# Windowed attention layers on one core: values spread through device memory, the band on small tiles, and new orders on three engines

## Chip, core and metric

The kernel runs on one core of a Trainium2 chip. The metric is device time in microseconds (us). Five engines run side by side, each in the order of its own program, and wait for one another by semaphores: TensorE (PE; its weight loads are listed as PEld), VectorE (DVE), ScalarE (ACT), GpSimd (POOL) and SyncE (SP), which issues the transfers.

## What is computed

2048 tokens of 128 channels go through a time-mixing layer with a norm, and then through six layers of windowed attention and a gated feed-forward net, all in float32, with a last norm behind:

```python
for i in range(DEPTH):                                    # 6
    x = attn_layer(shift_tokens(x), Wqkv[i], q_scale[i], k_scale[i], Wo[i]) + x
    x = ffn_layer(shift_tokens(x), ln_g[i], ln_b[i], W1[i], b1[i], W2[i], b2[i]) + x

def attn_layer(x, Wqkv, qs, ksc, Wo):                     # 16 heads of 64
    q, k, v = split(x @ Wqkv)
    q = l2norm(q) * qs;  k = l2norm(k) * ksc
    q = q * cos * scale + rotate_half(q) * sin * scale
    k = k * cos * inv   + rotate_half(k) * sin * inv
    # windows of 32 tokens; a query sees its own window and the one before
    sim = where(mask, -max, einsum('bhwie,bhwje->bhwij', bq, bk2) * 8)
    out = einsum('bhwij,bhwje->bhwie', softmax(sim), bv2)
    return out @ Wo
```

`bk2` and `bv2` hold, for each window of 32, the 32 tokens before it and its own 32: each key and value is wanted in two places.

## The kernel before

The tokens are cut into 16 tiles of 128. `layers` runs 96 tile-layers as a software pipeline. In step `s` four tiles are under way: `p = s + 1` (projections, norms of q and k, rotation), `a = s` (transposes of q and k, scores, softmax), `b = s - 1` (product with the values, output projection), and, for a pair of tiles in two steps, the feed-forward net. A step is **even** or **odd** by `s`: an odd step starts with the gating (`gelu`, `hidden`) and ends with the narrowing (`xa`) and the deviation of the norm (`dev_made`, line 1363); an even step ends with the norm's transposes (line 1372) and the widening (line 1262). Steps 7 to 94 are a loop of 44 rounds, each an odd and an even step.

Every engine's order is written out by hand in its own `step` function; nothing is scheduled by a tool. Operands pass through four pairs of PSUM banks: `bank_a` (queries, then values, of `p`), `bank_b` (keys, then the feed-forward), `bank_s` (probabilities, product with the values, output projection) and `bank_t` (transposes of q and k, scores). In the profile they are named `proj_a`, `proj_b`, `att`, `turn`.

The steps that the prediction follows:
- TensorE, in this order: probabilities turned (1246, `att<-identity,probs`), query projection (1278), key projection (1293), q transposes (1246, `turn<-identity,rotated`), product with the values (1312), k transposes (1246), `heads_out` turned (1246), the band (1332) and on top of it the scores (1338), value projection (1350), and behind it what is left of the step, with the output projection (1379).
- VectorE: sum of the masses (1187), in odd steps `hidden` (1196), the two sums of squares (1155), `heads_out` (1161), the inverse root (nine operations on 128x32, lines 88 to 104), `unit[0]` and `unit[1]` (1180), the two centrings of the scores (1169 and 1172), `xa` (1219), `xb` (1223), `var_f` (1228), `along[1]` (1233).
- GpSimd: `turns`, the shifted inputs, then `across[0]` (999), `along[0]` (1032), `rotated[0]` (1006), `across[1]`, in odd steps `rstd_f` (1040), `rotated[1]`. The k transposes of the next step wait for `rotated[1]`.
- ScalarE: the evacuations `p_t`, `q_t`, `k_t`, `o_t`, the squares, the value copy `val` (1114) and the exponentials (1061, `weigh`).
- SyncE: `spread(m, odd)` copies the values of tile `m` from `v_tok` (in the profile `val`) into `v_win`, where each window has its two blocks of 32 tokens, with sixteen transfers of 32 rows (lines 945 and 948). The next layer's weights are loaded from the same queue, between the spreads.

The band is a mask of 0 and -1e30 in bfloat16, 64 columns for each of the 16 heads, which TensorE writes into the scores' banks by a product with the identity; the first tile of the sequence has a mask of its own.

Of the kernel before, what the change touches and what calls it, by code (L numbers as in the profile page):

```python
# [23 lines left out]
F32 = mybir.dt.float32  # L24
# [101 lines left out]
def build(nc, x, vectors, mix_w1, mix_w2, decay_w1, decay_w2, r_weights, r_norm, wqkv, wo, ffn, qk_scales,  # L126
          positions, carry, ident, band, level_masks, out):
    with ExitStack() as ctx:
# [688 lines left out]
def layers(nc, ctx, given):  # L817
# [10 lines left out]
    passed = given["passed"]  # L828

    with ExitStack() as own:  # L830
# [44 lines left out]
        eps_set = sem("eps_set")  # L875
        cleared, centre_made = sem("cleared"), sem("centre_made")
# [12 lines left out]
        v_laid, v_spread = sem("v_laid"), sem("v_spread")  # L889
        scored, maxed, centred, weighed = sem("scored"), sem("maxed"), sem("centred"), sem("weighed")  # L890
# [39 lines left out]
        with nc.Block() as block:  # L930
            @block.sync
            def _(sp):
                def spread(m, odd):

                    now, old = v_tok[odd], v_tok[1 - odd]
                    sp.wait_ge(v_laid, m + 1)
                    stand_alone(sp, passed)
                    after(sp, mixed, 2 * (m - 1))
                    stand_alone(sp, passed)
                    for par in range(2):  # L940
                        base = 2 * WINDOW * par
                        own_rows = slice(base + WINDOW, base + 2 * WINDOW)
                        flat = [v[:, par, :, :].rearrange("p a e -> p (a e)") for v in (now, old)]
                        for w in range(BLOCKS):
                            sp.dma_start(v_win[odd][own_rows, w, :],
                                         flat[0][WINDOW * w:WINDOW * w + WINDOW, :]).then_inc(v_spread, 16)
                            before = flat[0][WINDOW * (w - 1):WINDOW * w, :] if w else flat[1][TILE - WINDOW:TILE, :]
                            sp.dma_start(v_win[odd][base:base + WINDOW, w, :], before).then_inc(v_spread, 16)
# [6 lines left out]
                sp.wait_ge(cleared, 2)  # L955
                for m in range(5):
# [90 lines left out]
            def _(act):  # L1047
                def step(s, h, odd, live):
# [8 lines left out]
                    def weigh(par):  # L1057
                        act.wait_ge(centred, 2 * a + par + 1)
# [20 lines left out]
                    if live["a"]:  # L1079
                        for j in range(2):  # L1080
# [3 lines left out]
                                .then_inc(q_laid, 1)  # L1084
                    if live["a"]:
# [5 lines left out]
                    if live["down"]:  # L1091
                        after(act, warmed, h)
                        act.activation(warm[:, :], ones[:, 0:1], ACT.Exp).then_inc(warmed, 1)
# [454 lines left out]
```

## Time and profile before

| | |
|---|---|
| median of 3 runs | 2002.96 us (2001.11 to 2008.23) |
| profiled execution, its own time | 2001.63 us |
| its span, first to last instruction | 1999.8 us |
| mean granted TensorE clock | 0.975 |
| busy: PE / DVE / ACT / POOL | 1771.6 / 1543.1 / 1156.1 / 1454.8 us |
| share of the span | 89% / 77% / 58% / 73% |

The first 195 us are the time-mixing layer, the last 15 us the last norm; in between are the 96 tile-layers, and from 262 us to about 1955 us the pairs of steps repeat. The chain of work that ended last covers only the last norm, 1% of the span, so it doesn't tell what sets the pace of the layers: the waits and the timeline of one pair do. In a timeline row the columns are start, duration, engine, line, operation, result and operands, count; in brackets stands the idle time of the engine just before, and what ended it. The duration of several matrix products in one row reaches to the end of the last one, which overlaps the next row's start. "issue" means that no releaser is seen.

### The profile page before, as it was taken

The page shows a single profiled execution, that of the slowest core. Times are in us where ns is not written, and L with a number is a line of the kernel's source. Part 1 is how long each engine was busy: PE and PEld are TensorE (multiplying, and loading weights), DVE is VectorE, ACT ScalarE, POOL GpSimd, SP SyncE. Part 2 cuts the span into 40 slices and gives each one's busy share as a digit, 9 for nine tenths or more (in the row PEclk, how much of TensorE's full clock was granted, in tenths as well). Part 3 has the DMA queues.
Part 4 walks back from the last instruction along what each step waited for, and adds up shares of the span by engine and source line. Part 5 has one row for each costly group of instructions (what it writes and reads, how often), then busy time and mean ns, then how long its engine had stood idle before and what let it go on. Part 6 is the DMA issues. An engine that isn't in the chain of part 4 may idle for free. (4 is left out here: it accounts for less than half of the span.)

```text
span 1999.8 us, 85355 instructions
## 1 busy us (share of the span) xinstructions
PE 1771.6 (89%) x34184; PEld 1277.4 (64%) x34184; DVE 1543.1 (77%) x2729; ACT 1156.1 (58%) x1966; POOL 1454.8 (73%) x967
## 2 busy tenths in 40 slices
PE   7764789999999999999999999999999999999995
PEld 3453466666666666666666666666666666666664
DVE  4774798778878877788788777887887788778864
ACT  2311456666666666666666666666666666666663
POOL 3221787787788778877887787778777877887771
PEclk9985899999999999999999999999999999999998
DMA  4000222223232223222223322233222232322220
GB/s 151 2 3 1 56 63 57 64 60 84 66 74 58 54 55 94 63 68 58 63 56 85 76 67 55 52 81 81 62 58 62 61 86 63 74 60 52 55 63 22
DMA packets 93581, 123.43 MB, mean 62 GB/s; under 512 B 27760, under 2 KB 41808, under 8 KB 93392
## 3 DMA queue, kind: packets, MB, share of 16 engines
q1 hardware_dynamic: 93232, 122.42, 24.3%
q8 instruction: 46, 0.75, 0.2%
q10 hardware_dynamic: 288, 0.13, 0.0%
q14 instruction: 15, 0.12, 0.0%
HBM read 20.74 MB, written 1.05 MB: 11 GB/s over the span
## 5 line engine op out<-in xcount | busy, mean ns | idle before, releaser
L999 POOL TENSOR_TENSOR across<-unit,turns 128x1024 f32<-128x1024 f32 x192 | 497.4, 2591 | 275.5 <-issue 265.6
L1006 POOL TENSOR_TENSOR rotated<-along,across 128x1024 f32<-128x1024 f32 x192 | 495.7, 2582 | 14.2
L1155 DVE TENSOR_REDUCE sums<-squares 128x16 f32<-128x1024 f32 x192 | 234.0, 1219 | 177.9 <-ACT squares L1054 177.7
L1246 PE MATMUL turn<-identity,rotated 128*128 128x128 f32 x1536 | 204.7, 276 | 35.5 <-POOL rotated L1006 34.3
L1246 PEld LDWEIGHTS turn<-identity,rotated 128*128 128x128 f32 x1536 | 172.3, 141 | 98.0 <-issue 82.5
L1032 POOL TENSOR_TENSOR along<-unit,turns 128x1024 f32<-128x1024 f32 x96 | 228.0, 2375 | 0.0
L1350 PE MATMUL proj_a<-w_qkv,shift_a 128*128 128x512 f32 x384 | 189.5, 616 | 36.3 <-DVE unit L1180 30.1
L1114 ACT COPY val<-proj_a 128x1024 f32<-128x1024 f32 x96 | 97.2, 1012 | 180.7 <-PE proj_a L1350 180.7
L1379 PE MATMUL att<-o_t,w_o 128*128 128x128 f32 x1536 | 188.9, 277 | 0.0
L1278 PE MATMUL proj_a<-w_qkv,shift_a 128*128 128x512 f32 x384 | 184.4, 603 | 5.0 <-POOL shift_a L989 3.7
L1379 PEld LDWEIGHTS att<-o_t,w_o 128*128 128x128 f32 x1536 | 181.0, 193 | 1.0 <-issue 1.0
L1089 ACT COPY k_t<-turn 128x512 f32<-128x512 f32 x192 | 103.2, 589 | 134.5 <-PE turn L1246 134.5
L1293 PE MATMUL proj_b<-w_qkv,shift_a 128*128 128x512 f32 x384 | 180.9, 593 | 0.0
L1233 DVE TENSOR_TENSOR along<-unit,turns 128x1024 f32<-128x1024 f32 x96 | 165.7, 1726 | 0.0
L1054 ACT ACTIVATE squares<-proj_a 128x1024 f32<-128x1024 f32 x96 | 98.2, 1023 | 115.8 <-PE proj_a L1278 115.8
L1312 PE MATMUL att<-v_win,p_t 64*32 64x64 f32 x12288 | 154.2, 225 | 0.8 <-ACT p_t L1074 0.8
L1338 PEld LDWEIGHTS turn<-k_t,q_t 64*32 64x32 f32 x12288 | 128.3, 105 | 41.4 <-issue 41.1
L1074 ACT COPY p_t<-att 128x512 f32<-128x512 f32 x192 | 103.1, 589 | 89.0 <-PE att L1246 89.0
L1312 PEld LDWEIGHTS att<-v_win,p_t 64*32 64x32 f32 x12288 | 135.6, 105 | 20.1 <-issue 16.9
L1161 DVE TENSOR_TENSOR heads_out<-att,inv_mass 128x512 f32<-128x512 f32 x192 | 123.6, 686 | 31.4 <-PE att L1312 31.4
L1338 PE MATMUL turn<-k_t,q_t 64*32 64x64 f32 x12288 | 144.2, 225 | 0.0
L1172 DVE TENSOR_TENSOR logits<-turn,row_max 128x512 f32<-128x512 f32 x192 | 132.8, 692 | 6.7
(201 smaller groups left out, 3366.2 us busy)
## 6 DMA issues: line engine op xcount, KB each, us to landing
v_win<-val SPq DMA_DIRECT2D x1536, 64.0 KB, 2.0
w_qkv<-wqkv_dram SPq DMA_DIRECT2D x18, 512.0 KB, 3.9
w_o<-wo_dram SPq DMA_DIRECT2D x6, 512.0 KB, 4.7
where<-positions_dram SPq DMA_DIRECT2D x1, 2048.0 KB, 10.7
w_ffn<-ffn_dram SPq DMA_DIRECT2D x12, 170.5 KB, 2.3
w_ffn<-ffn_dram SPq DMA_DIRECT2D x6, 192.0 KB, 2.3
x_tok<-x_dram SPq DMA_DIRECT2D x4, 256.0 KB, 4.2
out_dram<-final SPq DMA_DIRECT2D x4, 256.0 KB, 2.4
```

The source lines that it names most:

```text
L999: pool.tensor_tensor(a[:, :, ::-1, :], u, table, ALU.mult).then_inc(acrossed[j], 1)
L1006: pool.tensor_tensor(rotated[j][:, :, :], along[j][:, :, :], across[j][:, :, :], ALU.add).then_inc(rotated_in[j], 1)
L1032: pool.tensor_tensor(along[0][:, :, :], unit[0][:, :, :], turns[mine][:, 0, :].unsqueeze(1).broadcast_to([128, HEADS, HEAD]), ALU.mult).th ...
L1155: dve.tensor_reduce(sums[:, j, :], squares[j][:, :, :], AX.X, ALU.add).then_inc(summed[j], 1)
L1233: dve.tensor_tensor(along[1][:, :, :], unit[1][:, :, :], turns[mine][:, 2, :].unsqueeze(1).broadcast_to([128, HEADS, HEAD]), ALU.mult).the ...
L1246: mm = pe.transpose(bank[:, TILE * (i % 4):TILE * (i % 4) + TILE], buffer[:, TILE * i:TILE * i + TILE], identity[:, :])
L1278: mm = pe.matmul(bank_a[:, half, :], shift_a[mine][:, :], w_qkv[:, 512 * half:512 * half + 512], start=True, stop=True)
L1293: mm = pe.matmul(bank_b[:, half, :], shift_a[mine][:, :], w_qkv[:, base:base + 512], start=True, stop=True)
L1312: mm = pe.matmul(bank_s[WINDOW * w:WINDOW * w + WINDOW, par, HEAD * a_:HEAD * a_ + HEAD], p_t[rows, a_, WINDOW * w:WINDOW * w + WINDOW], v ...
L1338: mm = pe.matmul(bank_t[WINDOW * w:WINDOW * w + WINDOW, par, HEAD * a_:HEAD * a_ + HEAD], q_t[rows, a_, WINDOW * w:WINDOW * w + WINDOW], k ...
L1350: pe.matmul(bank_a[:, par, :].rearrange("p (a e) -> p a e", a=PAIRS), shift_a[mine][:, :], values[:, par, :, :], start=True, stop=True).th ...
L1379: mm = pe.matmul(bank_s[:, 0, 0:TILE], w_o[:, a_, :], o_t[:, a_, :], start=(a_ == 0), stop=(a_ == PAIRS - 1))
```

## The change

- **Values.** `spread` writes the tile's values to a buffer in device memory, `v_rows` (32 + 2 x 128 rows, the odd tile's last 32 rows also at its top), waits until they are there, and reads them back with four transfers of 128 rows (of two heads' halves, near and own window) in place of the sixteen. A write waits until all reads of the spread before it have landed.
- **Band.** Eight products on tiles of 64 rows and 32 columns in place of two on 128x128. In even steps ScalarE first copies the mask in question into `band_now`, so that no address depends on a register; the mask for the first tile is laid out for both row halves.
- **Orders.** TensorE: the query projection goes ahead of the turned probabilities, the product with the values ahead of the q transposes, the output projection and the norm's transposes ahead of the value projection, the deviation ahead of the narrowing. VectorE: `heads_out` between the two sums of squares, `centre_scores(1)` between `unit[0]` and `unit[1]`, then `centre_scores(0)`; `along[1]` ahead of `xa` and `var_f`. ScalarE: `o_t` right behind `k_t`, then `norm_tok` and the table load; `weigh(1)` first, the value copy just ahead of `weigh(0)`.

The step range, the tiles under way in a step and the buffers' numbers stay. GpSimd's code is the same.

On TensorE, an even step ahead of the loop, before:

```order
L1246 MATMUL att<-identity,probs 128x128 x8
L1278 MATMUL proj_a<-w_qkv,shift_a 128x512 x2
L1293 MATMUL proj_b<-w_qkv,shift_a 128x512 x2
L1246 MATMUL turn<-identity,rotated 128x128 x8
L1312 MATMUL att<-v_win,p_t 32x64 x64
L1246 MATMUL turn<-identity,rotated 128x128 x8
L1246 MATMUL att<-identity,heads_out 128x128 x8
L1332 MATMUL turn<-band_bf,identity_bf 128x512 x2
L1338 MATMUL turn<-k_t,q_t 32x64 x64
L1350 MATMUL proj_a<-w_qkv,shift_a 128x512 x2
L1372 MATMUL att<-identity,norm_tok 128x128 x2
L1379 MATMUL att<-o_t,w_o 128x128 x8
```

The same step on TensorE in the changed kernel (its line numbers are its own):

```order
L1295 MATMUL proj_a<-w_qkv,shift_a 128x512 x2
L1269 MATMUL att<-identity,probs 128x128 x8
L1316 MATMUL proj_b<-w_qkv,shift_a 128x512 x2
L1327 MATMUL att<-v_win,p_t 32x64 x64
L1269 MATMUL turn<-identity,rotated 128x128 x16
L1269 MATMUL att<-identity,heads_out 128x128 x8
L1360 MATMUL turn<-band_now,identity_bf 32x512 x8
L1368 MATMUL turn<-k_t,q_t 32x64 x64
L1379 MATMUL att<-o_t,w_o 128x128 x8
L1388 MATMUL att<-identity,norm_tok 128x128 x2
L1396 MATMUL proj_a<-w_qkv,shift_a 128x512 x2
```

The product with the values is now the fourth group instead of the fifth, the output projection stands ahead of the value projection, and the query projection starts the step.

On VectorE, the end of the same step, from `unit[0]` on, before:

```order
L1180 TENSOR_TENSOR unit<-proj_a,inv_norm 128x1024
L1180 TENSOR_TENSOR unit<-proj_b,inv_norm 128x1024
L1169 TENSOR_REDUCE row_max<-turn 128x8
L1172 TENSOR_TENSOR logits<-turn,row_max 128x512
L1169 TENSOR_REDUCE row_max<-turn 128x8
L1172 TENSOR_TENSOR logits<-turn,row_max 128x512
L1223 TENSOR_TENSOR xb<-att,xa 128x128
L1233 TENSOR_TENSOR along<-unit,turns 128x1024
```

And in the changed kernel:

```order
L1201 TENSOR_TENSOR unit<-proj_a,inv_norm 128x1024
L1190 TENSOR_REDUCE row_max<-turn 128x8
L1193 TENSOR_TENSOR logits<-turn,row_max 128x512
L1201 TENSOR_TENSOR unit<-proj_b,inv_norm 128x1024
L1190 TENSOR_REDUCE row_max<-turn 128x8
L1193 TENSOR_TENSOR logits<-turn,row_max 128x512
L1242 TENSOR_TENSOR xb<-att,xa 128x128
L1248 TENSOR_TENSOR along<-unit,turns 128x1024
```

One centring has moved between the halves; behind them nothing moved in an even step.

The rest of the diff, cut to its core:

```diff
+    v_rows = nc.dram_tensor("v_rows", (WINDOW + 2 * TILE, INNER), F32, kind="Internal").ap()
...
                 def spread(m, odd):
-                    now, old = v_tok[odd], v_tok[1 - odd]
+                    at = WINDOW + TILE * odd
+                    flat = v_tok[odd][:, :, :, :].rearrange("p b a e -> p (b a e)")
                     sp.wait_ge(v_laid, m + 1)
                     stand_alone(sp, passed)
+                    after(sp, v_spread, 64 * m)
+                    stand_alone(sp, passed)
+                    sp.dma_start(v_rows[at:at + TILE, :], flat).then_inc(v_written, 16)
+                    if odd:
+                        sp.dma_start(v_rows[0:WINDOW, :], flat[TILE - WINDOW:TILE, :]).then_inc(v_tail, 16)
+                    sp.wait_ge(v_written, 16 * m + 16)
+                    stand_alone(sp, passed)
+                    if not odd:
+                        sp.wait_ge(v_tail, 8 * m + 16)
+                        stand_alone(sp, passed)
                     after(sp, mixed, 2 * (m - 1))
                     stand_alone(sp, passed)
                     for par in range(2):
-                        base = 2 * WINDOW * par
...
-                        for w in range(BLOCKS):
-                            sp.dma_start(v_win[odd][own_rows, w, :],
-                                         flat[0][WINDOW * w:WINDOW * w + WINDOW, :]).then_inc(v_spread, 16)
-                            before = flat[0][WINDOW * (w - 1):WINDOW * w, :] if w else flat[1][TILE - WINDOW:TILE, :]
-                            sp.dma_start(v_win[odd][base:base + WINDOW, w, :], before).then_inc(v_spread, 16)
+                        for near in range(2):
+                            base = 2 * WINDOW * par + WINDOW * near
+                            row = TILE * odd + WINDOW * near
+                            sp.dma_start(v_win[odd][base:base + WINDOW, :, :],
+                                         v_rows[row:row + TILE, 512 * par:512 * par + 512]
+                                         .rearrange("(w p) f -> p w f", p=WINDOW)).then_inc(v_spread, 16)
...
                     def weigh(par):
-                        act.wait_ge(centred, 2 * a + par + 1)
+                        act.wait_ge(centred, 2 * a + 2 - par)
...
+                    if live["a"] and not odd:
+                        which = (0 if a % TILES == 0 else 1) if isinstance(a, int) else (tile_of(a) + 15) // 16
+                        after(act, scored, 2 * (a - 1))
+                        act.copy(band_now[:, :], band_bf[:, which, :]).then_inc(band_set, 1)
...
                         act.wait_ge(v_projected, 2 * p + 2)
-                        after(act, v_spread, 256 * p)
+                        after(act, v_written, 16 * (p - 1))
+                        if mine:
+                            act.wait_ge(v_tail, 8 * (p - 1) + 16)
                         act.copy(v_tok[mine][:, :, :, :], ...).then_inc(v_laid, 1)
...
+                        band = (band_bf[:, mask_other, :] if odd else band_now[:, :]).unsqueeze(1)\
+                            .broadcast_to([128, PAIRS, 2 * WINDOW])
+                        if not odd:
+                            pe.wait_ge(band_set, a // 2 + 1 if isinstance(a, int) else h + 4)
                         pe.wait_ge(k_laid, 2 * a + 2)
-                        for par in range(2):
-                            pe.matmul(bank_t[:, par, :].rearrange("p (a c) -> p a c", a=PAIRS), identity_bf[:, :], band,
-                                      start=True, stop=False, skip_group_check=True)
+                        stand_alone(pe, passed)
+                        for w in range(BLOCKS):
+                            for par in range(2):
+                                rows = slice(HEAD * par, HEAD * par + HEAD)
+                                at = HEAD * par + (WINDOW if w else 0)
+                                pe.matmul(bank_t[WINDOW * w:WINDOW * w + WINDOW, par, :]
+                                          .rearrange("p (a c) -> p a c", a=PAIRS),
+                                          identity_bf[rows, at:at + WINDOW], band[rows],
+                                          start=True, stop=False, skip_group_check=True)
...
-    first = hidden | ((a < WINDOW) & (c < WINDOW))
+    first = hidden | ((a % (2 * WINDOW) < WINDOW) & (c < WINDOW))
```

## Rows read from the trace of the kernel before

**Rows 1.** Windows, 42 repeating pairs: start:end, length, busy time (count) of each engine.

```profile
core 0: us, PE busy (x) PEld busy (x) DVE busy (x) ACT busy (x) POOL busy (x), PEclk, DMA share, GB/s
334.22:1865.00 1530.78, 1424.52 (x27715) 1038.01 (x27714) 1231.82 (x2142) 969.27 (x1636) 1228.15 (x799) 1.00 0.27 66
```

**Rows 2.** Waits of TensorE in that stretch: us in total, times, longest.

```profile
PE proj_a L1350 <- DVE unit L1180: 27.1, 81, 0.5
PE att L1246 <- issue: 26.2, 42, 0.6
PE turn L1246 <- POOL rotated L1006: 23.8, 42, 0.6
```

**Rows 3.** Timeline of TensorE, one pair from an even step's k transposes.

```profile
1016.03 1.09 PE L1246 MATMUL turn<-identity,rotated 128*128 128x128 f32 x8 [0.58 <-POOL rotated L1006]
...
1018.04 0.60 PE L1332 MATMUL turn<-band_bf,identity_bf 128*128 x2
1018.57 1.48 PE L1338 MATMUL turn<-k_t,q_t 64*32 64x64 f32 x128
1020.28 1.96 PE L1350 MATMUL proj_a<-w_qkv,shift_a 128*128 128x512 f32 x4 [0.23 <-DVE unit L1180]
...
1022.29 1.95 PE L1379 MATMUL att<-o_t,w_o 128*128 128x128 f32 x16
1024.40 1.99 PE L1262 MATMUL proj_b<-normed,w_ffn 128*128 128x256 f32 x8 [0.16 <-ACT normed L1122]
...
1027.10 1.04 PE L1246 MATMUL att<-identity,probs 128*128 128x128 f32 x8
1027.97 1.88 PE L1278 MATMUL proj_a<-w_qkv,shift_a 128*128 128x512 f32 x4
1029.69 1.88 PE L1293 MATMUL proj_b<-w_qkv,shift_a 128*128 128x512 f32 x4
...
1032.37 1.62 PE L1312 MATMUL att<-v_win,p_t 64*32 64x64 f32 x128
...
1052.47 1.09 PE L1246 MATMUL turn<-identity,rotated 128*128 128x128 f32 x8 [0.56 <-POOL rotated L1006]
```

**Rows 4.** Timeline of VectorE in the same pair.

```profile
1026.00 1.21 DVE L1187 TENSOR_REDUCE mass<-probs 128x16 f32<-128x1024 f32 x1
...
1028.25 0.47 DVE L1196 SCALAR_TENSOR_TENSOR hidden<-turn,w_ffn,gelu 85x256 f32<-85x256 f32 x1
...
1034.18 1.29 DVE L1161 TENSOR_TENSOR heads_out<-att,inv_mass 128x512 f32<-128x512 f32 x2 [0.30 <-PE att L1312]
1035.39 0.18 DVE L88 SCALAR_TENSOR_TENSOR sums_min<-sums 128x32 f32<-128x32 f32 x1
...
1037.56 1.22 DVE L1180 TENSOR_TENSOR unit<-proj_a,inv_norm 128x1024 f32<-128x1024 f32 x1
...
1042.47 0.47 DVE L1219 SCALAR_TENSOR_TENSOR xa<-proj_b,w_ffn,xb 128x256 f32 x1
...
1045.13 1.98 DVE L1233 TENSOR_TENSOR along<-unit,turns 128x1024 f32<-128x1024 f32 x1
```

**Rows 5.** Timeline of GpSimd in two neighbouring odd steps.

```profile
1009.56 3.34 POOL L999 TENSOR_TENSOR across<-unit,turns 128x1024 f32<-128x1024 f32 x1
...
1043.68 2.36 POOL L1006 TENSOR_TENSOR rotated<-along,across 128x1024 f32<-128x1024 f32 x1
```

**Rows 6.** Timeline of ScalarE, the copies of the turned probabilities.

```profile
1027.73 1.07 ACT L1074 COPY p_t<-att 128x512 f32<-128x512 f32 x2
```

**Rows 7.** Groups by line in that stretch: busy us, mean ns, idle before, releaser.

```profile
L1155 DVE TENSOR_REDUCE sums<-squares 128x16 f32<-128x1024 f32 x168 | 204.9, 1220 | 149.1 <-ACT squares L1054 149.1
```

**Rows 8.** Timeline early in the layers, a root operation beside GpSimd.

```profile
235.83 0.66 DVE L88 SCALAR_TENSOR_TENSOR sums_min<-sums 128x32 f32<-128x32 f32 x1
...
235.70 0.74 POOL L1017 TENSOR_TENSOR turns<-where,scales 128x256 f32<-128x256 f32 x1
```

**Rows 9.** Transfers by line: count, KB each, median us from issue to landing.

```profile
x_tok<-x_dram SPq DMA_DIRECT2D x4, 256.0 KB, 4.2
out_dram<-final SPq DMA_DIRECT2D x4, 256.0 KB, 2.4
```

## What I predict, and why

> **What bounds the kernel now.** I read the windows first. In the stretch of 42 identical pairs of steps, 1530.78 us long, TensorE is busy 93% at a granted clock of 1.00, VectorE and GpSimd 80% each [rows 1]. One pair takes 36.45 us. Then the waits of TensorE in that stretch [rows 2]. It waits little, but in every step: the value projection for VectorE's first normalised half (27.1 us, 81 times), the turning of the probabilities at the head of an even step (26.2, 42 times), the k transposes of an even step for GpSimd (23.8, 42 times). So this is not one full engine but rings of work across engines that close every pair. The timeline shows the ring that matters here [rows 3 to 5]:
> - the k transposes of an even step start at 1016.03 and the next (odd) step starts at 1027.10: **R** = 11.07 us on TensorE;
> - from that start to the end of `unit[0]` on VectorE, 1037.56 + 1.22 = 1038.78: **X** = 11.68 us;
> - from there GpSimd's five large operations run back to back, and the next even step's k transposes start at 1052.47: **P** = 13.69 us.
>
> R + X + P = 36.44 us, which is the pair. A second ring is as tight: `unit[0]` releases the value projection, behind which everything up to the next step's start waits in TensorE's order. The first ring has about 0.2 us of slack to the second, the 0.23 us that the value projection waits at 1020.28. An edit pays only if both rings get shorter.
>
> **The change, part by part.**
>
> *TensorE's order.* The output projection and the norm's transposes move between the scores and the value projection. The second ring is cut: `unit[0]` now has some 2 us more before the value projection asks for it, and the probabilities turn behind the query projection (1.72 us, 1027.97 to 1029.69), which covers their wait for `xb`. What is late next is the first ring, so I price that one.
>
> R, from the rows of the even step [rows 3]: 11.07 less the value projection's wait of 0.23, and less the wait of the widening behind the output projection. From 1022.29 to 1024.40 are 2.11 us, while the output projection streams as many columns (16 x 128) as the value projection does (4 x 512), 1.75 us or a little over; I take 0.36 off, with 0.16 (what the row itself shows as idle) as the other end. The band gives back some more, next. The added standing-alone waits and the wait for `band_set` find their semaphores set long before (a 64-column copy on ScalarE, issued while it waits for the k transposes): nothing, or 0.1 us.
>
> *The band on small tiles.* Two 128x128 products of 512 columns take 0.53 us (1018.04 to 1018.57). Now there are eight of the same length on 64x32 tiles, two row halves by four column quarters. If they ran one after another they would take 8 x 0.26 = 2.1 us. The scores, on the same tiles, say that they don't: 128 records of 64 columns take 1.48 us, while at the output projection's pace (1.75 us for 2048 columns) they would take 7.0 us, so 4.7 run at a time. Eight by that share are 0.45 us, all eight at once 0.27 us. I take 0.30, nearer to the second, since the long streams leave time to load the next weights: 0.23 off. Ends: 0.27 and 2.1 us. The Trainium skill, "TensorE: Matmul & The Clock Gate", Part 3 (Measured speedup vs the span model), gives packed tiles the length of one product and about 4 ns for each further one, here an estimate of 0.24 us; by it R would be 0.06 us shorter.
>
> So R becomes 11.07 - 0.23 - 0.36 - 0.23 = 10.25 us.
>
> X, from the first instruction of the odd step, now the query projection: it takes 1.72, the turned probabilities 0.87 (1027.10 to 1027.97), the key projection 1.72; so the product with the values starts at 4.31, if `p_t` is there: ScalarE starts those copies 0.63 after the turning starts and takes 1.07 [rows 6], 1.72 + 0.63 + 1.07 = 3.42, in time. `heads_out` starts 1.81 after that product (1032.37 to 1034.18), at 6.12. From `heads_out` to `unit[0]` were 3.38 us; now the second sum of squares stands between, 1.22 [rows 7]. `unit[0]` ends at 6.12 + 3.38 + 1.22 + 1.22 = 11.94. X grows by 0.26: products come earlier, but a whole reduction moved behind them.
>
> P stays 13.69: GpSimd's code is untouched, and `along[1]` on VectorE still falls into its run. The rows show how these two collide: `along`, issued at 1045.13, ends 1.07 us after GpSimd's operation from 1043.68 ends, and an operation of GpSimd that starts under it takes 3.34 instead of 2.36 us [rows 4, 5]. That 1 us is in P before and after.
>
> Sum: 10.25 + 11.94 + 13.69 = 35.88 against 36.44, **0.56 us a pair**. The other parity's ring (odd to odd) has some 1.5 us of room: TensorE's odd remainder loses its waits too, and GpSimd's run there has no `rstd` in it.
>
> *VectorE's order.* With `centre_scores(1)` between the halves, `unit[1]` comes 1.3 us later; GpSimd needs it only after three operations (7 us). In an even step the k transposes now wait longer for GpSimd (about 2 us), so the nine small root operations meet GpSimd's last large one. The trace has that case at the start of the layers: the first root operation took 0.66 instead of 0.18 us, to the end of GpSimd's 0.74 us operation [rows 8]. Here this costs the even X 0.5 to 1.4 us, inside the room of that parity's ring. The Trainium skill, "SBUF — State Buffer", Who interferes with whom, states it as an exclusive lock between a VectorE instruction with two SBUF inputs and GpSimd; the trace agrees with 0.66 us. `xa` and `var_f` move behind `along[1]`, about 2 us later; `rstd` is asked for after GpSimd's fourth operation and `xa` by the next key projection, 0.4 us after it is there by my count. Nothing, with little margin.
>
> *ScalarE's order.* `o_t` ahead of `norm_tok` and of the table load, `weigh(1)` first, the value copy one place later: ScalarE has waits in every step, and the value copy must end before the next query projection. By the sum it does, with 0.4 us to spare. The q transposes now stand right before the k transposes, whose bank waits for the q copies: about 0.3 us, in the even step under GpSimd's wait, in the odd one in that ring's room.
>
> *Values by way of device memory.* Sixteen transfers of 64 KB become a write of 512 KB, in odd tiles a tail of 128 KB, a wait for both, and four reads of 256 KB. No row has this route. A 256 KB write took 2.4 us and a 256 KB read 4.2 us [rows 9]: the write up to 4.8, the reads at best side by side 4.2, at worst in series 16.8; 9 to 22 us with the issues. The value copy ends about 1 us after the projection's 1022.2; its product stands just ahead of the k transposes at 1052.47, some 27 us later. Hidden at either end, and SyncE has fewer issues than before. At the five layer changes the weights of the next layer queue behind the reads instead of behind sixteen issues: 0 to 2 us each. The Trainium skill, "DMA: Bandwidth & Descriptors", Anatomy of one DMA, speaks against such a detour: it names device memory the slowest target to confirm a write. No run here shows that alone.
>
> **Sum over the run.** About 46 pairs have the full work (42 in the stretch and two at either side); 46 x 0.56 = 26 us. The start of the layers and the drain I leave as they are, 3 us either way. The profiled execution took 2001.63 us (span 1999.8), so 1976; the median of the runs shown is 1.3 us above it: **1977 us**. The bounds of the terms (band 0.27 to 0.53, widening 0.16 to 0.36, X up to 0.3 either way) put the pair between 35.5 and 36.2, so 1960 to 1992.
>
> **Rivals.**
> - *Nothing left over.* The first ring had only 0.2 us of slack, so if the band keeps 0.5 us, the output projection needs its 2 us and the odd root also meets GpSimd's copies (0.3 us), the ring is again 36.4 to 36.6: 2000 to 2010. For it: X really does grow. Against: three waits on TensorE vanish.
> - *VectorE's tail misses its gap (slower).* In an even step `along[1]` is ready 4.91 (both centrings and both halves, 1037.56 to 1042.47) + 0.3 for `xb` = 5.2 us after `unit[0]` starts; GpSimd's third operation starts at 6.1 (1043.68). If it is later than that, from 0.9 us more on, it waits that operation out, to 8.5, and ends at 9.5; the sum of masses, the reciprocal and the gating follow, 2.72 (1026.00 to 1028.72), and only then may the odd key projection overwrite its bank, at 12.3. From it to the next `unit[0]` are 1.72 + 1.81 + 3.38 + 1.22 = 8.1, then 1.22 + 13.69, and some 2.5 of root work after GpSimd's end: 37.8 us a pair, 62 us more: 2065. For it: VectorE is 80% full and each of these waits is new. Against: 0.9 us are left.
> - *The small tiles run in series.* 1.2 to 1.8 us on R, which also uses up those 0.9 us: 37.4 to 38, 2045 to 2075. Against it: the scores' 4.7 at a time.
> - *The detour takes longer than a step.* Each write waits for the last reads to land, so past 18 us a step it sets the pace; at 22 us 43 a pair, 2300. Only reads in strict series do that.
> - *More room than counted.* If GpSimd and VectorE collide less, the pair falls to 35.2 or so: 1945.
>
> **How the numbers follow.** Forecast 63%; nothing left over 17%; the missed gap 8%; tiles in series 5%; the detour 2%; more room 5%. A measurement of this kernel tells about 0.5% (10 us) from no change. Faster by more: the forecast nearly whole and the last case, 67%. Within: 18%. Slower: 15%. The range leaves out the slow cases and the fastest: 1953 to 2012; the forecast's own is 1960 to 1992.
>
> **What would show it.** The value projection's and the turned probabilities' waits gone; the even k transposes waiting about 2 us for GpSimd and nothing else large on TensorE; a pair of 35.9 us; `heads_out` starting 6.1 us after the query projection; eight band products within 0.3 us; `along[1]` ending before GpSimd's `rotated[0]` begins in even steps. The forecast is wrong if the odd key projection waits for `hidden`, if the product with the values waits for a transfer, or if the even root ends so late that the other parity's ring sets the pair.

## The result

| | changed | before |
|---|---|---|
| median | 2070.78 us (2061.48 to 2072.32, 4 runs) | 2005.58 us (2001.11 to 2008.23, 4 runs) |
| span of the profiled execution | 2070.1 us | 1999.8 us |
| mean granted TensorE clock | 0.934 | 0.975 |

The changed kernel takes 1.0311 times the time of the one before (95% interval 1.0284 to 1.0337): it is **slower**. The forecast was 1977 us with a range of 1953 to 2012, faster at 0.67.

The starts of the key projections give a ledger of the 70.3 us between the two spans. They are counted from 0: number n makes the keys of tile n, and "step n" in this ledger and in the texts below means its start, although it runs in step n - 1 of the kernel's own count. Numbers 11 and 93, first in the changed kernel, then in the one before:

```profile
415.37 1.88 PE L1316 MATMUL proj_b<-w_qkv,shift_a 128*128 128x512 f32 x4
1955.73 1.88 PE L1316 MATMUL proj_b<-w_qkv,shift_a 128*128 128x512 f32 x4
```

```profile
391.03 1.88 PE L1293 MATMUL proj_b<-w_qkv,shift_a 128*128 128x512 f32 x4
1886.99 1.88 PE L1293 MATMUL proj_b<-w_qkv,shift_a 128*128 128x512 f32 x4
```

Up to step 0 are 8.3 us (206.5 instead of 198.2; the kernels below lie between 199 and 208 us there, for a reason that is not known). Steps 0 to 11 take 208.9 us instead of 192.8, 16.1 more. The 41 pairs from step 11 to step 93 take 1540.4 instead of 1496.0, 44.4 more (37.57 us a pair instead of 36.49 on average; most pairs of the kernel before take 36.46). The rest is 1.5. So there are two losses to explain, the pairs and the start. Every kernel has one profiled execution, so how much these parts vary from one execution to the next is not known.

**The pair.** Page of the changed kernel, groups of instructions (busy, mean ns; idle before, and releaser):

```profile
L1269 PE MATMUL turn<-identity,rotated 128*128 128x128 f32 x1536 | 241.5, 307 | 112.6 <-POOL rotated L1021 94.6
L1248 DVE TENSOR_TENSOR along<-unit,turns 128x1024 f32<-128x1024 f32 x96 | 224.7, 2341 | 0.0
L1316 PE MATMUL proj_b<-w_qkv,shift_a 128*128 128x512 f32 x384 | 184.3, 602 | 23.2 <-DVE hidden L1217 23.2
```

TensorE's waits have gathered in one place: 94.6 us for GpSimd ahead of the k transposes, 2.1 us in every even step, where there were several of at most 0.6 us in a pair [rows 2, 3]. The key projection waits for `hidden`, and `along` takes 2.34 us on average. The timeline of TensorE in one pair, changed kernel:

```profile
1019.69 1.09 PE L1269 MATMUL turn<-identity,rotated 128*128 128x128 f32 x8
1022.87 1.67 PE L1269 MATMUL turn<-identity,rotated 128*128 128x128 f32 x8 [2.08 <-POOL rotated L1021]
1024.33 1.91 PE L1269 MATMUL att<-identity,heads_out 128*128 128x128 f32 x8
1026.17 0.61 PE L1360 MATMUL turn<-band_now,identity_bf 64*32 64x512 bf16 x8
1026.58 1.50 PE L1368 MATMUL turn<-k_t,q_t 64*32 64x64 f32 x128
...
1034.42 1.88 PE L1295 MATMUL proj_a<-w_qkv,shift_a 128*128 128x512 f32 x4
1036.13 1.04 PE L1269 MATMUL att<-identity,probs 128*128 128x128 f32 x8
1037.71 1.95 PE L1316 MATMUL proj_b<-w_qkv,shift_a 128*128 128x512 f32 x4 [0.54 <-DVE hidden L1217]
```

Behind the wait the same eight transposes that took 1.09 us [rows 3] take 1.67, and those of `heads_out` 1.91 instead of 1.09, which the kernel before has here:

```profile
1016.98 1.09 PE L1246 MATMUL att<-identity,heads_out 128*128 128x128 f32 x8
```

The windows of these stretches say why (the column ahead of the DMA share is the granted clock):

```profile
1020.80:1022.80 2.00, 0.00 (x0) 0.00 (x0) 1.90 (x3) 0.80 (x3) 2.00 (x2) 1.00 0.90 180
1022.87:1024.33 1.46, 1.46 (x8) 1.46 (x9) 1.36 (x4) 0.59 (x1) 1.10 (x3) 0.62 0.01 3
1024.33:1026.17 1.84, 1.84 (x9) 1.51 (x8) 1.67 (x6) 1.17 (x2) 0.03 (x1) 0.50 0.00 0
1026.17:1028.02 1.85, 1.85 (x138) 1.55 (x137) 0.39 (x1) 1.18 (x3) 1.32 (x1) 0.87 0.00 0
1028.02:1034.42 6.40, 6.40 (x39) 4.99 (x36) 6.21 (x7) 3.93 (x6) 6.32 (x4) 1.00 0.02 10
```

TensorE idles, and then the granted clock falls to 0.50, the 1.2 GHz of its two levels, through the transposes and into the band. Before, it was 1.00 over the whole stretch [rows 1]. All 41 steady pairs of the changed kernel have this fall; the waits of 2.08 us behind them, at 1962.13 and 1997.58, have none. What it does further is on VectorE and GpSimd, same pair:

```profile
1028.14 0.69 DVE L1190 TENSOR_REDUCE row_max<-turn 128x8 f32<-128x512 f32 x1 [1.57 <-PE turn L1368]
...
1032.12 2.79 DVE L1248 TENSOR_TENSOR along<-unit,turns 128x1024 f32<-128x1024 f32 x1
```

```profile
1031.47 2.36 POOL L1021 TENSOR_TENSOR rotated<-along,across 128x1024 f32<-128x1024 f32 x1
```

VectorE waits 1.57 us for the late scores, `along[1]` is issued 0.65 us after `rotated[0]` has begun and ends 1.08 us behind its end, `hidden` is late, and the odd key projection waits 0.54 us. That is the slow rival's ring, at 37.57 us instead of its 37.8, but its trigger is the clock. So the first theory: **the gathered wait costs the clock, and the clock makes `along[1]` miss its gap.**

### The profile page after: what moved, and what is told of

Same layout as the page of the kernel before. It is cut to its first block and busy times, and to the rows that moved or that the text cites. A ratio compares the mean times of both kernels' runs of the same rounds, so it can differ in the third digit from the quotient of the medians.

```text
span 2070.1 us, 86199 instructions
## 1 busy us (share of the span) xinstructions
PE 1812.0 (88%) x34760; PEld 1319.7 (64%) x34760; DVE 1629.7 (79%) x2729; ACT 1181.2 (57%) x2014; POOL 1452.0 (70%) x967
## 5 line engine op out<-in xcount | busy, mean ns | idle before, releaser
L1269 PE MATMUL turn<-identity,rotated 128*128 128x128 f32 x1536 | 241.5, 307 | 112.6 <-POOL rotated L1021 94.6
L1269 PEld LDWEIGHTS turn<-identity,rotated 128*128 128x128 f32 x1536 | 185.4, 153 | 148.1 <-issue 108.3
L1248 DVE TENSOR_TENSOR along<-unit,turns 128x1024 f32<-128x1024 f32 x96 | 224.7, 2341 | 0.0
L1190 DVE TENSOR_REDUCE row_max<-turn 128x8 f32<-128x512 f32 x192 | 131.3, 684 | 84.6 <-PE turn L1368 84.6
L1379 PE MATMUL att<-o_t,w_o 128*128 128x128 f32 x1536 | 196.8, 281 | 0.0
L1295 PE MATMUL proj_a<-w_qkv,shift_a 128*128 128x512 f32 x384 | 182.7, 598 | 9.9 <-ACT val L1143 6.2
L1396 PE MATMUL proj_a<-w_qkv,shift_a 128*128 128x512 f32 x384 | 182.4, 597 | 6.1 <-issue 6.1
L1076 ACT ACTIVATE probs<-logits 128x512 f32<-128x512 f32 x192 | 121.4, 632 | 104.8 <-DVE logits L1193 104.7
L1327 PEld LDWEIGHTS att<-v_win,p_t 64*32 64x32 f32 x12288 | 127.4, 105 | 83.1 <-issue 83.1
L1098 ACT COPY q_t<-turn 128x512 f32<-128x512 f32 x192 | 103.2, 589 | 104.9 <-PE turn L1269 104.9
L1368 PEld LDWEIGHTS turn<-k_t,q_t 64*32 64x32 f32 x12288 | 143.6, 108 | 18.5 <-issue 14.3
```

The lines of the kernel that those rows point to most:

```text
L1190: dve.tensor_reduce(row_max[:, heads], scores, AX.X, ALU.max).then_inc(maxed, 1)
L1248: dve.tensor_tensor(along[1][:, :, :], unit[1][:, :, :], turns[mine][:, 2, :].unsqueeze(1).broadcast_to([128, HEADS, HEAD]), ALU.mult).the ...
L1269: mm = pe.transpose(bank[:, TILE * (i % 4):TILE * (i % 4) + TILE], buffer[:, TILE * i:TILE * i + TILE], identity[:, :])
L1295: mm = pe.matmul(bank_a[:, half, :], shift_a[mine][:, :], w_qkv[:, 512 * half:512 * half + 512], start=True, stop=True)
L1368: mm = pe.matmul(bank_t[WINDOW * w:WINDOW * w + WINDOW, par, HEAD * a_:HEAD * a_ + HEAD], q_t[rows, a_, WINDOW * w:WINDOW * w + WINDOW], k ...
L1379: mm = pe.matmul(bank_s[:, 0, 0:TILE], w_o[:, a_, :], o_t[:, a_, :], start=(a_ == 0), stop=(a_ == PAIRS - 1))
```

## Experiments

Each kernel is told by its edit; "changed" is the kernel after the change. Times are medians; ratios are to the kernel before, on the same chip.

**1. The wait filled** (changed):

```diff
+                    if live["a"] and not odd:
+                        pe.wait_ge(q_laid, 2 * a + 1)
+                        for i in range(12):
+                            pe.transpose(bank_t[:, 0, 0:TILE], identity[:, :], identity[:, :])
                     if live["a"]:
                         pe.wait_ge(rotated_in[1], a + 1)
```

> The changed kernel, with twelve more transposes (the identity by the identity, into the bank that the k transposes then overwrite) ahead of the k transposes of every even step, where TensorE otherwise waits 2.1 us for GpSimd. They add work and take nothing away. Theory (the new orders gather TensorE's waits into one, and behind it the granted clock falls to 1.2 GHz through the k transposes, the heads_out transposes and the band): the granted clock stays at 1.00, R falls from 11.55 to 10.0 to 10.3 us, along[1] gets back ahead of rotated[0], the key projection no longer waits for hidden, a pair takes 35.5 to 36.2 us, and the time is 1975 to 2010 us. Rival A (VectorE's new order misses its gap by itself; the clock only follows): the clock may stay up, but the key projection still waits for hidden and the pair stays above 37 us: 2040 to 2070. Rival B (the detour or the small band tiles slow TensorE): as the changed kernel, 2065 to 2075.

1984.76 us, 0.9889 (0.9854 to 0.9924), as the theory had it. TensorE in an even step, then `along[1]` on VectorE and `rotated[0]` on GpSimd:

```profile
1025.47 1.53 PE L1343 MATMUL turn<-identity 128*128 128x128 f32 x12 [0.24 <-ACT q_t L1098]
1027.25 1.09 PE L1269 MATMUL turn<-identity,rotated 128*128 128x128 f32 x8 [0.25 <-POOL rotated L1021]
1028.18 1.04 PE L1269 MATMUL att<-identity,heads_out 128*128 128x128 f32 x8
...
1037.18 1.88 PE L1295 MATMUL proj_a<-w_qkv,shift_a 128*128 128x512 f32 x4
```

```profile
1034.91 2.00 DVE L1248 TENSOR_TENSOR along<-unit,turns 128x1024 f32<-128x1024 f32 x1
```

```profile
1035.90 3.23 POOL L1021 TENSOR_TENSOR rotated<-along,across 128x1024 f32<-128x1024 f32 x1
```

The window of its steady stretch has the clock at 1.00:

```profile
418.00:1850.00 1432.00, 1393.24 (x27695) 1032.11 (x27694) 1247.62 (x2063) 946.51 (x1617) 1177.70 (x769) 1.00 0.39 102
```

The same orders, with work added, take 35.43 us a pair; `along[1]` is back at 2.00 us and starts 0.99 us ahead of `rotated[0]`, and no wait for `hidden` is left. Rival A falls: VectorE's order does not miss its gap by itself.

**2. Half the wait filled** (the same with six):

> The filled wait with six transposes instead of twelve: some 0.8 us of the 2.1 us are filled, in its first half, and about 1 us stays idle ahead of the k transposes. Theory (what brings the clock down is one long wait; waits of 1 us, as here and in the kernel with the heads_out transposes ahead, don't): clock at 1.00, pair 35.4 to 35.5 us, 1978 to 1995 us. Rival C (what counts is the idle time, so that half of it still brings the clock down at the worst moments): some pairs of 36.5 to 37.6 us, 2000 to 2060 us.

1989.98 us, 0.9925 (0.9898 to 0.9951); pair 35.43 us, clock 1.00. A wait of 0.88 to 0.92 us ahead of the k transposes is harmless here: none of 42 has the fall.

**3. The wait cut in two, no work added** (changed): the transposes of `heads_out` ahead of the k transposes.

```diff
+                    if live["b"]:
+                        pe.wait_ge(scaled_out, 2 * b + 2)
+                        for j in range(2):
+                            transposes(bank_s[:, j, :], heads_flat, j, o_turned)
                     if live["a"]:
                         pe.wait_ge(rotated_in[1], a + 1)
...
-                    if live["b"]:
-                        pe.wait_ge(scaled_out, 2 * b + 2)
-                        for j in range(2):
-                            transposes(bank_s[:, j, :], heads_flat, j, o_turned)
```

> The changed kernel with one exchange in TensorE's order: the transposes of heads_out stand ahead of the k transposes, so that TensorE's one wait of 2.1 us in the even step is cut into two, about 0.6 us for heads_out and 0.9 us for GpSimd. No work is added. Theory: no single long wait, so the granted clock stays at 1.00; the band then waits for the k copies (0.4 to 0.6 us), R 10.2 to 10.6 us, pair 35.7 to 36.3 us, 1975 to 2010 us. Rival A (VectorE's order alone): the key projection still waits for hidden, 2040 to 2070 us. Rival C (the clock falls by the sum of idle time in a step, however it is cut): the clock falls as in the changed kernel, 2055 to 2085 us.

2000.89 us, 0.9971 (0.9951 to 0.9991). The steady part is as expected, 35.65 us a pair at a clock of 1.00 with waits of 0.2 to 0.8 us. TensorE in an even step:

```profile
1033.60 1.09 PE L1269 MATMUL att<-identity,heads_out 128*128 128x128 f32 x8 [0.34 <-DVE heads_out L1182]
1034.89 1.09 PE L1269 MATMUL turn<-identity,rotated 128*128 128x128 f32 x8 [0.20 <-POOL rotated L1021]
1036.76 0.41 PE L1360 MATMUL turn<-band_now,identity_bf 64*32 64x512 bf16 x8 [0.77 <-issue]
```

The waits add up to 1.3 us here, where the changed kernel has one of 2.1. So the wait was cut and also became shorter, and rival C is weakened but not excluded. The start is another matter: this kernel's steps 0 to 11 took 222.7 us, 30 more than before, and used the gain up. Experiments 1 and 2 lost 24 and 21 us there. The start is taken up in 9 and 10.

**4. The detour undone** (changed; `spread` and its waits as before):

> The changed kernel with the values spread as before, by sixteen transfers from SBUF to SBUF; everything else as changed. Theory: the detour is hidden, so nothing moves: clock lower in the even k transposes as in the changed kernel, pair 37.5 us, 2060 to 2075 us. Rival A: the same. Rival B (the detour's traffic is what slows TensorE): the clock or the rates of the transposes come back, 1975 to 2010 us.

2016.6 us, 1.0037 (1.0017 to 1.0057). The theory said "nothing moves", and 54 us went. Was it the detour after all? The k transposes of four even steps in a row:

```profile
992.88 1.60 PE L1255 MATMUL turn<-identity,rotated 128*128 128x128 f32 x8 [1.83 <-POOL rotated L1009]
1030.75 1.91 PE L1255 MATMUL turn<-identity,rotated 128*128 128x128 f32 x8 [1.96 <-POOL rotated L1009]
1068.64 1.09 PE L1255 MATMUL turn<-identity,rotated 128*128 128x128 f32 x8 [1.96 <-POOL rotated L1009]
1104.12 1.09 PE L1255 MATMUL turn<-identity,rotated 128*128 128x128 f32 x8 [1.97 <-POOL rotated L1009]
```

Here the clock falls behind only 16 of 42 such waits, all of 1.8 to 2.0 us. A pair with the fall takes 37.9 us, one without 35.6. A wait of 1.79 us (at 556) has the fall and one of 2.03 us (at 813) has not, so the length of the wait alone does not decide. The changed kernel's slow pair is 0.3 us shorter (its product with the values ends earlier), and I formed a second theory: the fall comes at moments of its own, and a slow pair of 37.57 us happens to bring every next wait to such a moment again. In the changed kernel the k transposes do lengthen slowly, from 1.33 us at 421.77 to 1.97 us at 1624: the fall slides through them by 0.02 us a pair.

**5. More work in the slow pair** (changed):

```diff
                         pe.wait_ge(v_spread, 64 * b + 64)
                         stand_alone(pe, passed)
+                        if odd:
+                            for i in range(2):
+                                pe.transpose(bank_s[:, 0, 0:TILE], identity[:, :], identity[:, :])
```

> The changed kernel with two more transposes (identity by identity, 0.27 us, into the bank that the product then overwrites) ahead of the product with the values in every odd step, behind the key projection that waits for hidden: it adds work to the ring of a slow pair, like the 0.3 us by which that product is later without the detour, and takes nothing away. Theory (the clock falls behind the 2 us wait only if the wait meets it at the right moment; the changed kernel's slow pair of 37.57 us happens to bring every wait to the same moment): a slow pair takes 37.8 to 37.9 us, the next wait comes at another moment, and only some of the pairs are slow, as without the detour: 2015 to 2045 us, faster by added work. Rival D (the length of the wait alone decides, so that every pair is slow): every pair 37.84 us, 2078 to 2090 us.

2038.66 us, 1.0148 (1.012 to 1.0177): 32 us less than the changed kernel, by adding work. Slow pairs take 37.8 us, and the clock falls behind 24 of 42 waits of 2.1 us:

```profile
1083.80 1.82 PE L1269 MATMUL turn<-identity,rotated 128*128 128x128 f32 x8 [2.08 <-POOL rotated L1021]
1121.59 1.96 PE L1269 MATMUL turn<-identity,rotated 128*128 128x128 f32 x8 [2.09 <-POOL rotated L1021]
1159.40 1.09 PE L1269 MATMUL turn<-identity,rotated 128*128 128x128 f32 x8 [2.08 <-POOL rotated L1021]
```

Rival D falls. Of two equal waits one costs the clock and the next does not, and how often it happens has changed with the pair's length. What sets the moments is not shown.

**6. Both: wait filled, detour undone** (edits 1 and 4):

> Both edits of the earlier runs together: the twelve transposes in the even step's wait, and the values spread by sixteen transfers from SBUF to SBUF. Theory (the detour costs nothing in the steady stretch beyond what the clock does, and some 10 us in the first steps of the run, where TensorE waits for instructions): every pair 35.6 to 35.7 us, the key projection of step 11 some 10 us earlier than with the filled wait alone, 1970 to 1985 us. Rival B (the detour itself costs what undoing it gave, 54 us): 1930 to 1945 us.

1980.09 us, 0.985 (0.982 to 0.988); 35.64 us a pair. Without the wait, undoing the detour gives 5 us, not 54, and in the pairs it loses 0.2 us. Rival B falls.

**7. Each part alone.** The detour alone (before, with `spread` and its waits as changed):

> The kernel before with the values spread by way of device memory and nothing else of the change. Theory: TensorE's waits stay short and the clock at 1.00; the product with the values ends 0.2 to 0.3 us earlier, which the second ring takes back in part (0 to 0.2 us a pair), and the first ten steps lose 8 to 20 us: 1998 to 2022 us. Rival B (the detour costs 54 us): 2050 to 2065 us.

1987.24 us, 0.9888 (0.9856 to 0.992): better than the theory. The steady pair is 36.00 us against 36.46. In the kernel before, the product with the values takes 1.6 us and `heads_out` waits for it [rows 3, 4]; with the detour (first TensorE, then VectorE):

```profile
1035.96 1.49 PE L1327 MATMUL att<-v_win,p_t 64*32 64x64 f32 x128
```

```profile
1036.25 1.22 DVE L1170 TENSOR_REDUCE sums<-squares 128x16 f32<-128x1024 f32 x1 [0.32 <-ACT squares L1067]
1037.46 1.29 DVE L1176 TENSOR_TENSOR heads_out<-att,inv_mass 128x512 f32<-128x512 f32 x2
```

The product is 0.1 us shorter and `heads_out` starts 1.50 us behind its start instead of 1.81, waiting for nothing. Why the product runs faster was not settled; but in the steady stretch of all ten kernels with the detour it takes 1.48 to 1.49 us, and in the five without it 1.52 to 1.80.

The small band tiles alone (before, with the eight products and `band_now`):

> The kernel before with the band on small tiles and nothing else of the change. Theory (the small tiles give back 0.3 us a step, of which the first ring passes on what the second ring leaves it, 0.2 us, and the detour is not needed for it): clock at 1.00, pair 36.1 to 36.3 us, 1988 to 2002 us. Rival (the eight small products come in series): 2040 to 2075 us.

2012.32 us, 1.0026 (1.001 to 1.0043). The scores follow 0.23 us behind the band instead of 0.53, and the pair stays at 36.47 us, where the theory had 36.1 to 36.3. TensorE's waits from 420 to 1850 us:

```profile
PE proj_a L1363 <- DVE unit L1186: 49.5, 79, 0.8
PE att L1252 <- issue: 24.3, 39, 0.6
PE turn L1252 <- POOL rotated L1008: 22.1, 39, 0.6
```

The value projection's wait doubles, from 25.1 us in the same stretch before: the second ring takes all of it.

The small band tiles undone (changed, with two products of 128x128):

> The changed kernel with the band again as two products of 128x128 per step; everything else as changed. Theory: the small tiles give back what was counted, 0.2 to 0.3 us in each step at full clock, twice that behind the wait of the even step, and the clock still falls: 2070 to 2095 us. Rival B (the small tiles cost the time): 1975 to 2010 us. Rival A: 2070 to 2095 us.

2060.57 us, 1.0258 (1.0228 to 1.0288), below the 2070 to 2095 expected. The clock falls in 40 of 41 pairs, and the slow pair is 37.57 us to the hundredth as with them: in a slow pair the ring runs over `along[1]` and `hidden`, and the band does not lie on it.

**8. The orders alone** (changed, with edits 4 and the band undone):

> The changed kernel with the detour and the small band tiles undone: the new orders alone. Theory (the orders make the 2 us wait, and the clock falls behind some of the waits, with a slow pair near 37.9 us as without the detour): full-clock pairs of 35.9 to 36.1 us, at least a quarter of the pairs slow, 2010 to 2040 us. Rival B (detour and band bring the fall of the clock, the orders alone don't): clock at 1.00 in the steady stretch, 1980 to 2000 us.

2033.33 us, 1.0129 (1.0092 to 1.0166). The wait is there and the clock falls behind 27 of 43; pairs of 36.1 and 37.9 us. So the orders bring it, without the other two parts.

**9. The start: the first eleven tiles spread from SBUF to SBUF**, the later ones through device memory, on the kernel of experiment 1. `spread_near` holds the sixteen transfers of before, and SyncE waits there until they have landed; for the eleventh tile it also writes the values to device memory, for the first later one:

```diff
-                for m in range(5):
-                    spread(m, m % 2)
-                with sp.Fori(0, 5) as i:
-                    spread(i * 2 + 5, 1)
-                    spread(i * 2 + 6, 0)
+                for m in range(11):
+                    spread_near(m, m % 2)
+                with sp.Fori(0, 2) as i:
+                    spread(i * 2 + 11, 1)
+                    spread(i * 2 + 12, 0)
```

> The changed kernel with the filled wait, and with the first eleven tiles of values spread from SBUF to SBUF as before; from the twelfth on by device memory. Theory (in the first ten steps the detour's transfers delay the loading of instructions): the key projection of step 11 comes 8 to 18 us earlier than with the filled wait alone, the pairs stay at 35.4 us, 1962 to 1977 us. Rival (the new orders are what stalls the start): as with the filled wait alone, 1980 to 1990 us.

1963.27 us, 0.979 (0.9756 to 0.9825). Steps 0 to 11 take 200.8 us instead of 216.9; the pairs stay at 35.43. **This kernel beats both**: it is faster than the kernel before beyond its interval, though whether by 2% is open. On the kernel of experiment 3:

> The changed kernel with the transposes of heads_out ahead of the k transposes, which cuts the long wait in two without added work, and with the first eleven tiles of values spread from SBUF to SBUF. Theory: the pairs stay at 35.65 us at full clock, and the start, where TensorE waits for instructions while the detour's transfers run, gets back 12 to 22 us: 1975 to 1990 us. Rival (the new orders stall the start by themselves): as without the second edit, 1995 to 2005 us.

1990.91 us, 0.9915 (0.9882 to 0.9947): 10 us gained, where the theory had 12 to 22 at the start. Its steps 0 to 11 take 216.2 us instead of 222.7, so with this order most of the start's loss stays, and the detour is not its main part. In its profile the granted clock is 0.95 even in busy stretches, so its stretches compare only roughly with the others'.

**10. The same edit on the changed kernel itself:**

> The changed kernel, its 2 us wait left as it is, with the first eleven tiles of values spread from SBUF to SBUF and the later ones by device memory. Theory (the start and the steady pairs lose separately: the first eleven steps lose some 16 us because the detour's transfers run while TensorE waits for its instructions, and the pairs lose to the clock): steps 0 to 11 take 196 to 203 us instead of 208.9, the waits of TensorE that the profile puts on nothing there fall from 25.9 to about 14 us, the pairs stay at 37.57 us, 2052 to 2064 us. Rival (the start is lost to the new orders and the band): steps 0 to 11 as in the changed kernel, 2065 to 2075 us.

2052.66 us, 1.025 (1.0198 to 1.0303): 18 us less by the medians, though its interval overlaps that of the changed kernel. The two spans differ by 21.3 us, 10.6 at the start and 10.6 in the pairs. Steps 0 to 11 take 198.3 us instead of 208.9, and TensorE's waits of over 0.7 us there that the profile puts on nothing ("issue") add up to 16.5 us instead of 26.0 (5.8 in the kernel before). One of them in both kernels, in the middle of the product with the values, the changed kernel first:

```profile
259.78 0.72 PE L1327 MATMUL att<-v_win,p_t 64*32 64x64 f32 x53
263.88 0.30 PE L1327 MATMUL att<-v_win,p_t 64*32 64x64 f32 x3 [3.38 <-issue]
```

```profile
257.74 1.45 PE L1353 MATMUL att<-v_win,p_t 64*32 64x64 f32 x125
260.36 0.30 PE L1353 MATMUL att<-v_win,p_t 64*32 64x64 f32 x3 [1.17 <-issue]
```

The product stops 3 instructions short of its end, at a place where no semaphore is waited for, for 3.38 and 1.17 us. These stops stand in the steps ahead of the loop and in its first rounds, and not later. That fits instructions still on their way behind the detour's transfers, but that is argued, not shown. Nor is it the whole: with the detour alone steps 0 to 11 take 197.2 us, with the orders alone 192.7, with orders and detour but the old band 210.2. It needs both; which order matters was not tried.

The pairs did not stay as they were, as the theory had it: five of the 41 are without the fall. Three of its first waits:

```profile
444.89 1.09 PE L1295 MATMUL turn<-identity,rotated 128*128 128x128 f32 x8 [2.10 <-POOL rotated L1047]
480.32 1.09 PE L1295 MATMUL turn<-identity,rotated 128*128 128x128 f32 x8 [2.08 <-POOL rotated L1047]
515.78 1.77 PE L1295 MATMUL turn<-identity,rotated 128*128 128x128 f32 x8 [2.07 <-POOL rotated L1047]
```

TensorE's loop is the changed kernel's; what differs is the start ahead of it. The trace also answers a rival that was left open: that filling the wait helped only by the pair's new length. The five pairs here have that length, 35.41 to 35.47 us, with a wait of 1.8 to 2.1 us in them, and the fall came back after three of them and after two; in experiments 1 and 2 it stayed away through all 41.

## Why the prediction was wrong

- **The step that failed is R.** The prediction saw the 2 us wait coming and took it for a sign of being right ("waiting about 2 us for GpSimd and nothing else large"). It took every duration of R from rows at a clock of 1.00 [rows 1, 3], as if 2 us of idle time left TensorE's pace as it was. At full clock R is 9.93 us (experiment 1, 1027.25 to 1037.18; 10.25 forecast); behind the fall it is 11.55 (1022.87 to 1034.42).
- **The sum was sound at full clock.** X 11.98 (forecast 11.94), P 13.52 (13.69), the pair 35.43 (35.88).
- **The missed gap** was priced right, term by term: from `unit[0]` to the key projection 12.37 us (12.3 forecast), from there to the next `unit[0]` 7.94 (8.1), P 13.57 (13.69), the root work 2.47 (2.5), 37.57 in all with the 1.22 of `unit[0]` (37.8). It was weighed too low, at 8%. Its 0.9 us of margin were counted from a timetable in which the scores come in time, and they are there at full clock (0.99 in experiment 1); the clock takes 1.6 us of R and with it the margin. That the late scores could reach `along[1]` was told only of small tiles in series. The one cause eats the gain and opens the rival; they were counted as separate chances.
- **The start**, "3 us either way", lost 16 us, and 8 more up to step 0 have no known cause. A stretch that a change runs through for the first time was left out of the sum because no row of it was read with the change in mind.
- **The detour** was hidden in the steady stretch, as forecast, and more than that: alone it gives 0.46 us a pair (36.46 to 36.00), which the prediction did not have. **The small tiles** run side by side, as forecast (0.23 us where 0.30 was taken), and are worth nothing alone, because of the second ring, as told. The value projection's wait did vanish from the even steps.

The Trainium skill, "TensorE: Matmul & The Clock Gate", HAM oscillation, describes a loop of matrix products that waits some 3 to 5 us for a transfer in every round and starts every next round at the lower clock. The trace shows the same pattern, with 41 falls in 41 pairs, but behind waits of 2.1 us and with TensorE busy 92% of the time. The prediction used another part of that page and did not ask what its own 2 us wait would do.

## What to carry to other kernels

When a change moves waits of the fullest engine together, price the new wait as a risk to its clock, also where it lies off the critical path: look up what its neighbours' rows would be at half the pace, and whose margin that takes. Several short waits left the clock up here where one long one did not, though they were also less in sum (1.3 us against 2.1); filling or cutting the wait is a cheap test (experiments 1 and 3). Before a part is blamed because undoing it helps, see whether the pair's length alone has moved.

## What was not expected of the hardware

- A single wait of 2.1 us in a stretch that is otherwise busy brought the granted clock from 1.00 to 0.50 in the work behind it; the wait of 0.9 us in experiment 2 did not.
- The fall depends on when the wait comes: of waits of 2.1 us, 41 of the 42 in the changed kernel's steady part brought it and 24 of 42 in experiment 5. There 0.27 us of work added to a pair made the kernel 32 us faster.
- With values spread by 512 KB writes (2.8 us to landing) and 256 KB reads (4.8 us) the product that uses them took 1.49 us instead of 1.60 (experiment 7).
